# Self-attention of a decoder layer: ScalarE empties PSUM for VectorE, and the projections move to other steps

## The chip, the cores and the metric

One core of one Trainium2 chip. The metric is the device time of one execution of the whole program in microseconds: 2352.65 us, the median of three runs (2352.45 to 2359.95).

## The reference

A decoder layer of three sublayers: causal self-attention with rotary embedding, a cross-attention that gathers, and a quantised gated feed-forward, each followed by a layer norm without weights. Only self-attention is touched. In f32, with x of 4 batches, 1024 tokens, 256 channels and 16 heads of 64:

```
q = (x @ wq.T + bq)  split into 16 heads of 64;  k, v likewise
q, k = rope(q, k)                      # pairs of even and odd channels turned
scores = q k^T, -inf above the diagonal
attn = softmax(scores / 8)
out = (attn @ v) @ wo.T + bo
x = layernorm(x + out)
```

## The kernel before

The work of self-attention (`attention`, L110) is cut into 16 groups (4 batches by 4 groups of 4 heads), and a group into two pairs of heads; there are 32 pairs n, and p = n % 2 is the pair's place in its group i. p = 0 is called the even pair, p = 1 the odd one. The two heads of a pair lie on the two halves of the partitions.

For a pair TensorE computes, in f32, the transposed scores of 12 units of 128 keys by up to 512 queries (`scores`, L439), adds minus the row maximum by a one-row bf16 matmul (`shift`, L447), ScalarE takes the exponential into one of four buffers (`exponentials`, L543), GpSimd zeroes the part above the diagonal (`mask_probs`, L796) and adds the probabilities up for the denominators (`add_probs`, L814 and L817), and TensorE multiplies them by the values (`weigh`, L463). A pair has 6 steps m of two units each; `weigh` lags one step behind.

The row maximum must be known before. While pair n runs, TensorE computes the scores of pair n + 1 once more, untransposed, in 9 chunks of up to 512 columns per head (`max_chunk`, L417); VectorE adds a mask to the diagonal blocks (L664) and reduces each chunk (`maximum`, L670 and L675), combines and negates (`negate`, L681, L684), TensorE spreads the result into a row (`max_row`, L429) and ScalarE copies it to `bias` (`copy_row`, L532). That copy is where a pair begins in this text.

The projections for group i + 1 also run within group i: four q/k units in the even pair (`project_qk`, L360 to L364, three products of high and low f32r parts), two value units in the odd pair (`project_v`, L385 to L387), and the output projection of group i - 1 in the odd pair (`project_out`, L401). Every q/k unit is 128x1024 (even and odd channels, 512 tokens). VectorE adds the bias and multiplies by cosine and sine in four operations reading PSUM (`rotate`, L608) into `turned` and `crossed`; GpSimd subtracts and adds the two (`turn`, L833, L834); SP restacks `turned` by DMA into the operands of the next pair (`stack`, L280). VectorE copies the values out with their bias (`values`, L649) and adds the output projection to y (`residual`, L711). Weights and x are loaded into three `raw` buffers (L266) and split by VectorE into high and low parts (`split`, L614, L616). The denominators go through PSUM (`sums`, L475), a ScalarE copy (L557) and two DMAs that ScalarE issues (L562), are inverted by VectorE and broadcast by SP, and VectorE normalises (`normalise`, L697).

What orders this: each engine's queue is written out by hand over n and m, with the same tables CHUNKS_AT (which chunks in which step) and FULL_AT (which projection in which step). PSUM has a ring of three slots of two banks, taken in the order of `slot_order`, and a separate slot for the outputs. A use of a slot waits until the use three places earlier has been read (`wait_slot`):

```
            elif kind == "max":
                pe.wait_ge(s_mread, PARTS * (NCH * n + u + 1))
            elif kind == "qk":
                pe.wait_ge(s_term, TERMS * (QK_UNITS * n + u + 1))
```

so a chunk's slot waits for VectorE's reduction and a q/k unit's for VectorE's rotation, a score's for its exponential, the row's for ScalarE's copy.

Of the kernel before, what the change touches and what calls it, by code (L numbers as in the profile page):

```python
# [17 lines left out]
P = 128  # L18
# [13 lines left out]
CHUNKS = [[(0, 0), (2, 0)], [(3, 0)], [(1, 0), (5, 1)], [(4, 0)], [(5, 0)], [(6, 0)], [(7, 0)], [(4, 1), (6, 1)], [(7, 1)]]  # L32
# [3 lines left out]
CHUNKS_AT = [range(0, 0), range(0, 3), range(3, 5), range(5, 7), range(7, 9), range(0, 0)]  # L36
# [36 lines left out]
def slot_order():  # L73

    order = [("qk", 0, u) for u in range(QK_UNITS)] + [("v", 0, u) for u in range(V_UNITS)]
    order += [("max", 0, c) for c in range(NCH)] + [("row", 0, 0)]
    for n in range(PAIRS):
        i, p = divmod(n, 2)
        for m in range(STEPS):
            order += [("s", n, 2 * m), ("s", n, 2 * m + 1)]  # L80
            if n + 1 < PAIRS:
                order += [("max", n + 1, c) for c in CHUNKS_AT[m]]
# [6 lines left out]
            if m == 1 and n:  # L89
                order.append(("den", n - 1, 0))  # L90
            if m == STEPS - 1 and n + 1 < PAIRS:
                order.append(("row", n + 1, 0))
# [4 lines left out]
def split_order():  # L97

    order = [("x", 0, piece) for piece in range(X_PIECES)] + [("qk", 1, kt) for kt in range(KT)]
    for i in range(GROUPS):  # L100
        if i + 1 < GROUPS:
            order.append(("v", i + 1, 0))
        if i + 2 < GROUPS:
            order += [("qk", i + 2, kt) for kt in range(KT)]
# [5 lines left out]
def attention(nc, dram, y, psum):  # L110

    ctx = ExitStack()
    with ctx:
# [13 lines left out]
        bv = sb("bv", [P, GC])  # L127
# [10 lines left out]
        crossed = [sb(f"crossed{n}", [P, 2, BANK]) for n in range(2)]  # L138
# [3 lines left out]
        vals = [sb(f"vals{n}", [P, TT, GH, D]) for n in range(2)]  # L142
        maxes = sb("maxes", [P, 2, TT + TT // 2])
# [13 lines left out]
        out_bias = sb("out_bias", [P, E])  # L157
        a_stats = sb("a_stats", [P, TT, 6])
# [16 lines left out]
        s_bv = sem("bv_loaded")  # L175
# [6 lines left out]
        s_qk_done = sem("qk_projected")  # L182
        s_term = sem("rotary_terms")
# [3 lines left out]
        s_m = sem("max_scores")  # L187
        s_mmask = sem("max_chunks_masked")
# [35 lines left out]
        def wait_slot(pe, kind, n, u):  # L224
# [28 lines left out]
        def _(sp):  # L253
# [14 lines left out]
            def load_v_bias(i):  # L268

                if i:  # L270
                    sp.wait_ge(s_vals, V_UNITS * i)
# [67 lines left out]
        def _(pe):  # L339
# [145 lines left out]
            for c in range(NCH):  # L485
                max_chunk(0, c)
# [1854 lines left out]
```

## Time and profile before

| | us |
|---|---|
| median of the runs | 2352.65 |
| the profiled execution | 2353.15 |
| its span, first to last instruction | 2351.4 |
| self-attention, up to about | 1500 |
| mean granted TensorE clock | 0.907 of full |

Busy over the span: TensorE 81%, VectorE 66%, GpSimd 58%, ScalarE 39%. "Idle before" an instruction is the time its engine stood still ahead of it, and the arrow names the instruction that released it. The fraction PEclk is the granted clock of TensorE, 1.00 being 2.4 GHz and 0.5 being 1.2 GHz. Matmul ends are modelled, so a stretch of TensorE is best read from start to start.

### The profile page before, as it was taken

How to read it: one execution, taken by the hardware profiler on the slowest of the kernel's cores; microseconds unless marked ns; L12 is line 12 of the kernel's file. 1: busy time of each engine (PE TensorE's matmuls, PEld its weight loads, DVE VectorE, ACT ScalarE, POOL GpSimd, SP SyncE). 2: the span in 40 equal slices, each digit the busy share in tenths (PEclk: the TensorE clock that was granted, in tenths of full speed). 3: DMA queues.
4: the chain of work that ended last, by engine and by line, in shares of the span. 5: the costliest groups of instructions: out<-in, count | busy, mean ns of one | idle time of the engine just before them, and what ended most of it. 6: DMA issues, size and time to landing. Idle time of an engine off the chain costs nothing. (4 is left out here: it accounts for less than half of the span.)

```text
span 2351.4 us, 41565 instructions
## 1 busy us (share of the span) xinstructions
PE 1910.8 (81%) x16891; PEld 1149.5 (49%) x16891; DVE 1551.9 (66%) x2339; ACT 912.5 (39%) x1273; POOL 1352.3 (58%) x1066
## 2 busy tenths in 40 slices
PE   6898988898879889887998888658788788784575
PEld 3444445445445454444454454436566566563332
DVE  5666665656766656666557664167868868768676
ACT  0222222222222222222222223137675765874375
POOL 2666656756846766766568466235555454646247
PEclk8999989999989999998999999779898898998786
DMA  7022112212221221222122111200000000100002
GB/s 209 19 53 50 48 46 57 61 35 55 62 50 48 53 50 48 52 52 59 32 57 61 32 48 33 66 6 8 2 3 7 2 2 2 41 3 2 2 1 72
DMA packets 59087, 93.34 MB, mean 40 GB/s; under 512 B 25360, under 2 KB 37648, under 8 KB 54928
## 3 DMA queue, kind: packets, MB, share of 16 engines
q1 hardware_dynamic: 49680, 90.41, 15.4%
q8 instruction: 134, 2.20, 0.4%
q10 hardware_dynamic: 9216, 0.27, 0.2%
q14 instruction: 57, 0.47, 0.1%
HBM read 52.37 MB, written 4.46 MB: 24 GB/s over the span
## 5 line engine op out<-in xcount | busy, mean ns | idle before, releaser
L817 POOL TENSOR_TENSOR acc<-acc,probs 128x1024 f32<-128x1024 f32 (+3 forms) x320 | 567.5, 1774 | 103.6 <-ACT probs L543 74.8
L543 ACT ACTIVATE probs<-psum 128x1024 f32<-128x1024 f32 (+3 forms) x384 | 291.2, 812 | 611.4 <-PE psum L447 610.5
L670 DVE TENSOR_REDUCE maxes<-psum 128x2 f32<-128x1024 f32 (+1 forms) x224 | 268.4, 1223 | 197.0 <-PE psum L417 187.2
L439 PE MATMUL psum<-operands 64*128 64x512 f32 (+3 forms) x1536 | 327.2, 537 | 26.9 <-DVE maxes L675 23.4
L1375 ACT ACTIVATE onehot<-psum 128x1024 bf16<-128x1024 f32 x320 | 323.9, 1041 | 1.3 <-PE psum L1185 1.3
L463 PE MATMUL psum<-probs,vals 128*64 128x512 f32 (+3 forms) x1536 | 291.9, 501 | 17.2 <-issue 12.8
L1203 PE MATMUL psum<-pieces,onehot 128*128 128x64 bf16 x7680 | 287.3, 198 | 22.9 <-ACT vs L1382 16.9
L1203 PEld LDWEIGHTS psum<-pieces,onehot 128*128 128x128 bf16 x7680 | 258.9, 101 | 84.8 <-issue 44.9
L1782 POOL TENSOR_TENSOR vs<-vs,wgt 128x1280 f32<-128x1280 f32 x64 | 156.3, 2442 | 247.0 <-DVE wgt L1626 246.9
L814 POOL COPY acc<-probs 128x1024 f32<-128x1024 f32 x64 | 67.9, 1062 | 331.6 <-ACT probs L543 331.6
L439 PEld LDWEIGHTS psum<-operands 64*128 64x128 f32 x1536 | 133.9, 192 | 172.7 <-issue 104.6
L664 DVE TENSOR_TENSOR psum<-psum,later 128x512 f32<-128x512 f32 (+1 forms) x160 | 94.0, 587 | 184.5 <-PE psum L417 184.5
L1185 PE MATMUL psum<-i0T,near 32*128 32x512 bf16 x640 | 130.4, 407 | 83.3 <-ACT onehot L1375 77.3
L1592 DVE TENSOR_TENSOR prod<-psum,xq 128x320 f32<-128x320 f32 x256 | 124.2, 489 | 108.3 <-PE psum L1203 102.9
L796 POOL TENSOR_SCALAR_AFFINE_SELECT probs<-probs 128x256 f32<-128x256 f32 x256 | 123.4, 498 | 105.6 <-ACT probs L543 105.1
L463 PEld LDWEIGHTS psum<-probs,vals 128*64 128x64 f32 x1536 | 95.2, 137 | 164.2 <-issue 141.2
L401 PE MATMUL psum<-wo,ctxT 128*128 128x256 f32 x512 | 145.9, 448 | 34.4 <-DVE maxes L675 22.8
L557 ACT ACTIVATE rden<-psum 128x1024 f32<-128x1024 f32 x32 | 32.8, 1025 | 360.7 <-PE psum L475 360.7
L1382 ACT ACTIVATE vs<-psum 128x320 f32<-128x320 f32 x256 | 115.5, 451 | 144.8 <-DVE prod L1592 144.2
L417 PE MATMUL psum<-operands 64*128 64x512 f32 (+3 forms) x768 | 113.0, 398 | 53.2 <-DMA operands<-turned 46.0
L401 PEld LDWEIGHTS psum<-wo,ctxT 128*128 128x128 f32 x512 | 114.2, 229 | 61.6 <-DVE maxes L675 26.0
L417 PEld LDWEIGHTS psum<-operands 64*128 64x128 f32 x768 | 62.6, 195 | 136.8 <-issue 64.1
(222 smaller groups left out, 3315.6 us busy)
## 6 DMA issues: line engine op xcount, KB each, us to landing
operands<-turned SPq DMA_DIRECT2D x124, 256.0 KB, 4.4
rden<-inverse_rows SPq DMA_DIRECT2D x64, 256.0 KB, 3.9
raw<-in_wqk SPq DMA_DIRECT2D x30, 256.0 KB, 5.2
y<-in_x SPq DMA_DIRECT2D x1, 4096.0 KB, 18.8
wo<-in_wo SPq DMA_DIRECT2D x16, 256.0 KB, 2.6
out<-res SPq DMA_DIRECT2D x16, 256.0 KB, 2.1
raw<-in_wv SPq DMA_DIRECT2D x15, 256.0 KB, 5.0
raw<-in_xT SPq DMA_DIRECT2D x12, 256.0 KB, 3.6
```

The costliest lines, as they stand in the source:

```text
L401: last = nc.tensor.matmul(dst[:, t // 2, (t % 2) * E:(t % 2 + 1) * E], ctxT[:, ct, tok:tok + P], wo[:, ct, :], start=ct == 0, stop=ct == C ...
L417: last = nc.tensor.matmul(dst[:, hh, col:col + width], ops[p][rows, 0, qt * P:(qt + 1) * P], ops[p][rows, 1, hf * BANK:hf * BANK + width], ...
L439: nc.tensor.matmul(dst[:, hh, 0:width], ops[n % 2][rows, 1, kt * P:(kt + 1) * P].bitcast(F32), ops[n % 2][rows, 0, a:a + width].bitcast(F3 ...
L463: last = nc.tensor.matmul(obank[rows, hf, a - hf * BANK:BANK], vals[i % 2][:, kt, 2 * p + hh, :], probs[u % PBUF][:, hh, 0:width], start=k ...
L543: nc.scalar.activation(probs[u % PBUF][:, :, 0:width], slot("s", n, u)[:, :, 0:width], ACT.Exp, scale=1.0 / D ** 0.5).then_inc(s_exp, 1)
L670: V.reduce_max(maxes[:, :, place_of[0]:place_of[-1] + 1:step], src[:, :, 0:len(parts) * width].rearrange("p h (k q) -> p h k q", q=width), ...
L817: G.tensor_tensor(dst, dst, src, ALU.add).then_inc(s_acc, 1)
L1185: last = nc.tensor.matmul(bc[m % 2][:, hf * BANK:(hf + 1) * BANK], near[row:row + Q, NK * j + k, :], i0T[row:row + Q, hp // 2, :], start=T ...
L1203: last = nc.tensor.matmul(out, onehot[:, n % 2, k, tok:tok + P], pieces[b % 2][p][:, h, :, :].rearrange("p (s c) d -> p s (c d)", s=2), st ...
L1375: A.activation(onehot[:, n % 2, k, :], bc[m % 2], ACT.Relu).then_inc(s_oh, 1)
L1592: V.tensor_tensor(prod[u % 2][:, :, :].rearrange("p t (k d) -> p t k d", d=HD), slot("s", n, u)[:, :, 0:W].rearrange("p t (k d) -> p t k d ...
L1782: G.tensor_tensor(v, v, w.broadcast_to([P, TT * NK * 2, HD]), ALU.mult).then_inc(s_wm, 1)
```

## The change

- ScalarE copies every max chunk from PSUM to one of three bf16 buffers in SBUF (`copy_chunk`), every q/k unit to one of two f32 buffers (`stage`), and the values (`values`). The PSUM slots are released by these copies. VectorE masks and reduces the bf16 copies, and rotates out of the staged copy, writing the sine terms back in place; `crossed` is gone.
- The value bias is no longer added to the values: once, at the start, it is multiplied by all of wo (8 matmuls) and added to the output bias. The load of the value bias for each group is gone; the start loads all of wo (1 MB) and spreads the bias over 128 columns.
- q/k units run in steps 0, 1, 4, 5 of the even pair (before 1, 2, 3, 4), values in steps 4, 5 of the odd pair (before 2, 3). In step 1 the chunks come behind projection and sums. The chunks with a masked block come first; steps 1 to 4 have 2, 2, 2, 3 of them.
- GpSimd turns q/k unit 3 at the head of the odd pair. VectorE splits the q/k weights in step 0 and the value weights in step 1 of the odd pair (before steps 4 and 0). Projections wait only for the half of x that they read; at a batch change three pieces of x are loaded in one place and the fourth behind the next stack of operands.

```
-CHUNKS = [[(0, 0), (2, 0)], [(3, 0)], [(1, 0), (5, 1)], [(4, 0)], [(5, 0)], [(6, 0)], [(7, 0)], [(4, 1), (6, 1)], [(7, 1)]]
+CHUNKS = [[(0, 0), (2, 0)], [(3, 0)], [(1, 0), (5, 1)], [(4, 1), (6, 1)], [(7, 1)], [(4, 0)], [(5, 0)], [(6, 0)], [(7, 0)]]
-CHUNKS_AT = [range(0, 0), range(0, 3), range(3, 5), range(5, 7), range(7, 9), range(0, 0)]
+CHUNKS_AT = [range(0, 0), range(0, 2), range(2, 4), range(4, 6), range(6, 9), range(0, 0)]
-FULL_AT = [[None, ("qk", 0), ("qk", 1), ("qk", 2), ("qk", 3), None],
-           [("out", 0), ("out", 1), ("v", 0), ("v", 1), None, None]]
+FULL_AT = [[("qk", 0), ("qk", 1), None, None, ("qk", 2), ("qk", 3)],
+           [("out", 0), ("out", 1), None, None, ("v", 0), ("v", 1)]]
+CHUNKS_LAST = 1
+MBUF = 3
...
             elif kind == "max":
-                pe.wait_ge(s_mread, PARTS * (NCH * n + u + 1))
+                pe.wait_ge(s_mcopy, NCH * n + u + 1)
...
             elif kind == "qk":
-                pe.wait_ge(s_term, TERMS * (QK_UNITS * n + u + 1))
+                pe.wait_ge(s_stage, QK_UNITS * n + u + 1)
...
+            def copy_chunk(n, c):
+                k = NCH * n + c
+                act.wait_ge(s_m, k + 1)
+                if k >= MBUF:
+                    act.wait_ge(s_mread, PARTS * (k + 1 - MBUF))
+                nc.scalar.activation(chunks[k % MBUF][:, :, :], slot("max", n, c)[:, :, :], ACT.Copy).then_inc(s_mcopy, 1)
+            def stage(i, u):
+                m = QK_UNITS * i + u
+                act.wait_ge(s_qk_done, m + 1)
+                if m >= 2:
+                    act.wait_ge(s_rot, TURNS * (m - 1))
+                nc.scalar.activation(staged[m % 2][:, :, :], slot("qk", i, u)[:, :, :], ACT.Copy).then_inc(s_stage, 1)
+            def values(i, u):
+                act.wait_ge(s_v_done, V_UNITS * i + u + 1)
...
+            def project_value_bias():
+                pe.wait_ge(s_bv, 16 * (NG + 1))
+                pe.wait_ge(s_bvr, 1)
+                wait_slot(pe, "bias", 0, 0)
+                dst = slot("bias", 0, 0)
+                for k in range(NG * CT):
+                    last = nc.tensor.matmul(dst[:, 0, 0:E], bv_rep[:, k, :], wo_all[:, k, :],
+                                            start=k == 0, stop=k == NG * CT - 1)
...
-                for dst, x, b, table in ((tu[:, 0, :], ev, be, cosE), (tu[:, 1, :], od, bo, cosO),
-                                         (co[:, 0, :], od, bo, sinE), (co[:, 1, :], ev, be, sinO)):
+                for dst, x, b, table in ((tu[:, 0, :], ev, be, cosE), (tu[:, 1, :], od, bo, cosO)):
                     V.scalar_tensor_tensor(out=dst, in0=x, scalar=b, in1=table[:, tok], op0=ALU.add, op1=ALU.mult)\
+                     .then_inc(s_term, 1)
+                dve.wait_ge(s_term, TERMS * m + 2)
+                for x, b, table in ((ev, be, sinO), (od, bo, sinE)):
+                    V.scalar_tensor_tensor(out=x, in0=x, scalar=b, in1=table[:, tok], op0=ALU.add, op1=ALU.mult)\
                      .then_inc(s_term, 1)
...
+                    if p == 1 and m == 0 and i + 1 < GROUPS:
+                        turn(i + 1, QK_UNITS - 1)
                     for u in (2 * m, 2 * m + 1):
                         if u in DIAGONAL:
                             mask_probs(n, u)
```

## Rows read from the trace of the kernel before

**Rows 1.** The page: busy time over the span.

```profile
PE 1910.8 (81%) x16891; PEld 1149.5 (49%) x16891; DVE 1551.9 (66%) x2339; ACT 912.5 (39%) x1273; POOL 1352.3 (58%) x1066
```

**Rows 2.** Busy time by stretch: even pair, odd pair, batch change, start; clock, DMA.

```profile
core 0: us, PE busy (x) PEld busy (x) DVE busy (x) ACT busy (x) POOL busy (x), PEclk, DMA share, GB/s
501.48:543.85 42.37, 37.48 (x218) 19.51 (x218) 30.89 (x40) 12.01 (x16) 32.10 (x28) 1.00 0.21 54
543.85:590.21 46.36, 42.05 (x250) 24.06 (x251) 28.83 (x46) 12.12 (x16) 26.15 (x22) 0.93 0.21 46
681.67:734.70 53.03, 40.69 (x218) 21.83 (x218) 39.48 (x48) 12.01 (x16) 33.77 (x28) 0.87 0.25 63
0.00:51.11 51.11, 30.15 (x106) 16.45 (x106) 32.25 (x47) 1.29 (x2) 11.79 (x18) 0.85 0.73 215
```

**Rows 3.** Timeline of TensorE in the even pair: start us, us, instruction, idle before.

```profile
510.32 0.47 PE L360 MATMUL psum<-xT_high,wqk_high 128*128 128x512 f32 x1 [1.75 <-DVE maxes L675]
...
543.18 0.64 PE L429 MATMUL psum<-ident,negmax 128*64 128x128 bf16 x16 [2.00 <-DVE crossed L608]
```

**Rows 4.** Timeline of TensorE in an odd pair, two stalls.

```profile
459.68 3.72 PE L401 MATMUL psum<-wo,ctxT 128*128 128x256 f32 x16
...
469.33 5.20 PE L401 MATMUL psum<-wo,ctxT 128*128 128x256 f32 x16 [1.65 <-DVE maxes L675]
...
498.44 0.49 PE L439 MATMUL psum<-operands 64*128 64x128 f32 x4 [1.47 <-DVE maxes L675]
```

**Rows 5.** Timeline of TensorE behind the 2.00 us stall.

```profile
543.75 3.11 PE L439 MATMUL psum<-operands 64*128 64x512 f32 x8
```

**Rows 6.** Timeline of TensorE, step 3 of the even pair and the next scores.

```profile
522.76 1.99 PE L439 MATMUL psum<-operands 64*128 64x512 f32 x8
...
527.64 0.50 PE L360 MATMUL psum<-xT_high,wqk_high 128*128 128x512 f32 x1
...
530.57 1.77 PE L439 MATMUL psum<-operands 64*128 64x512 f32 x8
```

**Rows 7.** ScalarE: 128x1024 from PSUM (busy us, mean ns); issue of the two DMAs.

```profile
L543 ACT ACTIVATE probs<-psum 128x1024 f32<-128x1024 f32 x186 | 184.0, 1024 | 419.6 <-PE psum L447 419.6
...
516.27 1.13 ACTq L562 DMA_DIRECT2D dcol<-rden  x2
```

**Rows 8.** VectorE: chunk maximum and rotation terms by shape.

```profile
L670 DVE TENSOR_REDUCE maxes<-psum 128x2 f32<-128x1024 f32 x192 | 229.3, 1223 | 193.7 <-PE psum L417 187.2
...
L608 DVE SCALAR_TENSOR_TENSOR crossed<-psum,bqk,rot 128x512 f32<-128x512 f32 x128 | 89.6, 742 | 0.0
```

**Rows 9.** Timeline of VectorE: operations from SBUF, without and beside GpSimd.

```profile
31.97 0.69 DVE L616 TENSOR_TENSOR xT_low<-acc,xT_high 128x512 fp32r<-128x512 f32 x1
...
49.74 0.20 DVE L684 TENSOR_SCALAR negmax<-maxes 128x16 bf16<-128x16 f32 x1
...
504.32 1.21 DVE L697 TENSOR_TENSOR ctxT<-osum,rden 128x1024 f32<-128x1024 f32 x1
...
539.19 1.25 DVE L684 TENSOR_SCALAR negmax<-maxes 128x16 bf16<-128x16 f32 x1
...
545.54 1.63 DVE L616 TENSOR_TENSOR wv_low<-raw,wv_high 128x512 fp32r<-128x512 f32 x1
```

**Rows 10.** Timeline of GpSimd at the same times.

```profile
534.77 4.36 POOL L817 TENSOR_TENSOR acc<-acc,probs 128x1024 f32<-128x1024 f32 x2
539.09 1.28 POOL L833 TENSOR_TENSOR turned<-turned,crossed 128x512 f32<-128x512 f32 x1
...
545.19 1.44 POOL L833 TENSOR_TENSOR turned<-turned,crossed 128x512 f32<-128x512 f32 x1
546.59 1.72 POOL L834 TENSOR_TENSOR turned<-turned,crossed 128x512 f32<-128x512 f32 x1
```

**Rows 11.** Timeline at a batch change: the stack's issue on SP, the chunk on TensorE.

```profile
687.48 3.64 SPq L280 DMA_DIRECT2D operands<-turned  x4
...
695.83 1.76 PE L417 MATMUL psum<-operands 64*128 64x128 f32 x10 [8.01 <-DMA operands<-turned]
```

More of the change, by code:

```diff
@@ L75, in slot_order @@
     order = [("qk", 0, u) for u in range(QK_UNITS)] + [("v", 0, u) for u in range(V_UNITS)]
-    order += [("max", 0, c) for c in range(NCH)] + [("row", 0, 0)]
+    order += [("max", 0, c) for c in range(NCH)] + [("bias", 0, 0), ("row", 0, 0)]
     for n in range(PAIRS):
@@ L79, in slot_order @@
         for m in range(STEPS):
+            chunks = [("max", n + 1, c) for c in CHUNKS_AT[m]] if n + 1 < PAIRS else []
             order += [("s", n, 2 * m), ("s", n, 2 * m + 1)]
-            if n + 1 < PAIRS:
-                order += [("max", n + 1, c) for c in CHUNKS_AT[m]]
+            if m != CHUNKS_LAST:
+                order += chunks
             if FULL_AT[p][m]:
@@ L90, in slot_order @@
                 order.append(("den", n - 1, 0))
+            if m == CHUNKS_LAST:
+                order += chunks
             if m == STEPS - 1 and n + 1 < PAIRS:
@@ L100, in split_order @@
     for i in range(GROUPS):
+        if i + 2 < GROUPS:
+            order += [("qk", i + 2, kt) for kt in range(KT)]
         if i + 1 < GROUPS:
             order.append(("v", i + 1, 0))
-        if i + 2 < GROUPS:
-            order += [("qk", i + 2, kt) for kt in range(KT)]
         if i % NG == 2 and i // NG + 1 < B:
@@ L137, in attention @@
         turned = sb("turned", [P, 2, 2, S])
-        crossed = [sb(f"crossed{n}", [P, 2, BANK]) for n in range(2)]
+        staged = [sb(f"staged{n}", [P, 2, BANK]) for n in range(2)]
         ops = [sb(f"operands{n}", [P, 2, S], F32R) for n in range(2)]
@@ L142, in attention @@
         vals = [sb(f"vals{n}", [P, TT, GH, D]) for n in range(2)]
+        chunks = [sb(f"chunks{n}", [P, 2, BANK], BF16) for n in range(MBUF)]
         maxes = sb("maxes", [P, 2, TT + TT // 2])
@@ L486, in _ @@
                 max_chunk(0, c)
+            project_value_bias()
             max_row(0)
@@ L515, in _ @@
                         sums(n - 1)
+                    if m == CHUNKS_LAST and n + 1 < PAIRS:
+                        for c in CHUNKS_AT[m]:
+                            max_chunk(n + 1, c)
                     if m == STEPS - 1 and n + 1 < PAIRS:
@@ L563, in spread_sums @@
                        .then_inc(s_dcol, 16)
+            for u in range(QK_UNITS):
+                stage(0, u)
+            for u in range(V_UNITS):
+                values(0, u)
+            for c in range(NCH):
+                copy_chunk(0, c)
             copy_row(0)
             for n in range(PAIRS):
+                i, p = divmod(n, 2)
                 for m in range(STEPS):
@@ L571, in _ @@
                         copy_out(n - 1, 1)
+                    if m != CHUNKS_LAST and n + 1 < PAIRS:
+                        for c in CHUNKS_AT[m]:
+                            copy_chunk(n + 1, c)
+                    if FULL_AT[p][m] and i + 1 < GROUPS:
+                        kind, u = FULL_AT[p][m]
+                        if kind == "qk":
+                            stage(i + 1, u)
+                        if kind == "v":
+                            values(i + 1, u)
                     if m == 1 and n:
                         spread_sums(n - 1)
+                    if m == CHUNKS_LAST and n + 1 < PAIRS:
+                        for c in CHUNKS_AT[m]:
+                            copy_chunk(n + 1, c)
                     if m == 3:
@@ L733, in _ @@
                 rotate(0, u)
-            for u in range(V_UNITS):
-                values(0, u)
             for piece in range(X_PIECES):
@@ L769, in _ @@
                             rotate(i + 1, u)
-                        if kind == "v" and i + 1 < GROUPS:
-                            values(i + 1, u)
+                    if m == CHUNKS_LAST and n + 1 < PAIRS:
+                        for c in CHUNKS_AT[m]:
+                            maximum(n + 1, c)
                     if p == 1 and m == STEPS - 1 and i % NG == 2 and i // NG + 1 < B:
-                        for piece in range(2):
+                        for piece in range(KT):
                             split_x(i // NG + 1, piece)
                     if p == 0 and m == 0 and i % NG == 3 and i // NG + 1 < B:
-                        for piece in range(2, X_PIECES):
+                        for piece in range(KT, X_PIECES):
                             split_x(i // NG + 1, piece)
```

106 lines of the change are left out of this document (58 added, 48 removed).

## The prediction

> **What bounds the kernel now.** I read the page first: TensorE is busy 81% of the span, ScalarE 39% [rows 1]. The change lies wholly in self-attention, so the next view is busy time by stretch, between the copies of the maximum row (L532) with which each head pair begins [rows 2]. A pair that projects q and k for the next group (an even pair) takes 42.37 us, with TensorE busy 37.48. The odd one after it, with output and value projections, takes 46.36 us, busy 42.05 at a mean clock of 0.93. VectorE and GpSimd are busy about 30 us of each, ScalarE 12. TensorE is the bound, and it stands still 4.9 and 4.3 us of the two pairs. A group of two pairs lasts 88.73 us; 15 groups project for a successor.
>
> TensorE's timeline shows where it stands. In the even pair the first projection waits 1.75 us for VectorE's maximum of the chunk in its PSUM slot, and the maximum row waits 2.00 us for the rotation of the last q/k unit, whose slot it reuses [rows 3]. In the odd pair an output projection waits 1.65 us and a score 1.47 us, again for maxima [rows 4]. So every larger stall is a PSUM slot that VectorE has not read. Idleness also costs clock: behind the 2.00 us stall eight score matmuls take 3.11 us [rows 5] where the same eight take 1.77 elsewhere [rows 6], which is half clock (1.2 instead of 2.4 GHz) for a few us. The output projection behind the 1.65 us stall takes 5.20 us [rows 4], one before it 3.7. With the shift behind the scores (0.4) that is 1.3 + 0.4 + 1.5 = 3.2 us of a group.
>
> **The floor.** Without stalls the even pair is its busy time, 37.5. The odd one is 42.05 less 3.2 of slow clock, 38.9. Floor 76.4 us for a group.
>
> **ScalarE's new work and what it makes late.** Nine chunk copies, on average two q/k stages and one value copy come to a pair: 12 copies of 128x1024 from PSUM at 1.02 us [rows 7], 12.3 us on top of 12, so 24 of 40: no bound by amount. But its queue is in order, and TensorE's slots now hang on it. Take time from the end of the second projection (step 1, even pair). The sums take 1.94 us; ScalarE copies them by 2.97, then issues two DMAs, 1.13 us [rows 7], and copies the first chunk by 5.15. TensorE has run sums, two chunks (1.02) and one score (0.9) by 3.86, and its second score needs that chunk's slot: stall 1.3. The exponentials of that step end near 8.45, TensorE wants their slot at 8.2: 0.25. In step 4 q/k unit 2 waits for the copy of the chunk three places ahead: 0.45. Sum 2.0 us a pair, odd pairs likewise. Steps 2 and 3 keep no projection: 7.81 us less 2.93 leaves 4.9 [rows 6], against 4.1 us of ScalarE. The maximum row's slot is now that of an exponential and is free; the copies of the last stage and of the row (2.04 us) lie beside row and scores (2.4). So 76.4 + 4.0 = 80.4 us a group.
>
> **VectorE and GpSimd.** Values leave VectorE (1.2 us each). A maximum reads bf16 in SBUF instead of PSUM, 1.23 us now [rows 8]; I take no more than 0.1 off. The rotation is the doubtful part. Its four operations now take 0.74 us reading PSUM and a table [rows 8]; changed, they read two SBUF tensors. The trace has no such operation; the nearest row is the split's subtraction of the same 128x512, 0.69 us with GpSimd idle [rows 9]. Yet beside GpSimd the same shape takes 1.63 us, and GpSimd's turns 1.44 and 1.72 instead of 1.28 [rows 9, 10]. And a 16-element scaling, 0.20 us alone, takes 1.25: it ends just after the GpSimd turn that began before it [rows 9, 10]. So where both want SBUF, one waits for the other's instruction to end. The change puts 16 rotation terms a group into this conflict.
>
> Price: GpSimd has 32 us in an even pair [rows 2]; 16 rotation terms add at most 0.57 each, 9 us, masks and normalisation 2.5: 43.5 us, begun 3 us into the pair. GpSimd turns unit 3 at the head of the next pair, before it masks that pair's first probabilities. TensorE wants those masks 7.6 us into the odd pair (step 0: scores and shift 2.1, products 0.8, output projection 3.7; step 1: scores and shift 1.1), 47.4 us from the even pair's start, with 39.8 for that pair. Every lock collected: 46.5, plus the mask 0.8 and idleness in step 2, 49 to 51; and VectorE (last chunk reduced and negated by 36.9, unit 2 rotated between GpSimd's additions by 41.6, normalised by 43.9, unit 3 by 47.8) has two splits of q/k weights (2.2 us alone, some 6 in turns with GpSimd) before the residual that frees the output slot: near 55 us where TensorE comes at 49.1. All locks: stall 6. No lock: unit 3 is staged 0.5 us into the odd pair, rotated by 3.3, turned by 5.9, masked by 6.7, in time: stall 0. GpSimd is busy three quarters of an even pair, and a term that meets it meets it anywhere in an instruction, so I take the middle, 3 us. A stall of this size had a half-clock stretch behind it before [rows 3, 5]: 1.6 us. Group 85.0 us, saving 3.7; 15 groups, 56 us.
>
> **Batch changes.** Three pairs of the kind of 681.7 to 734.7 take 53.0 instead of 42.4 us [rows 2]. The stack of operands is issued at 687.5 behind the loads of x, the chunk waits 8.01 us for it, and the pair runs at 0.87 of the clock [rows 11]. Now three pieces are loaded at a time when their buffers are free, the fourth behind the stack, and only units 2 and 3 need it. Its split falls between two rotations, 1 to 2 us. Saving 9 each, 27 us.
>
> **Start and end.** Before the first pair lie 51.1 us, VectorE busy 32 [rows 2]. Added: a stage copy 1 us, locks between rotations and turns 4, bias spreading 1.2, eight f32 matmuls and an addition 3.5, chunk copies and 1 MB more of DMA ahead of the operands 0 to 5; removed: values, 2.4. I take 8 longer, 3 to 14 as ends. The last two pairs gain 2. The bias loads that leave SP's queue were hidden, and the output bias is read a group later. The weights' loads change places (q/k before v), as their splits do; all have most of a pair to land, so nothing is counted, and if one were late, a projection would wait its 5 us.
>
> Sum: 56 + 27 + 2 - 8 = 77 us less. The profiled execution is 2353.15 us, 0.5 above the median of the three runs. Forecast 2276 us.
>
> **Rivals.**
> A, the port costs nothing on the path (0.22): turn and masks are in time, group 80.4, saving 125 + 27 + 2 - 8 = 146: 2207. For it: VectorE rests about 12 us of a pair, and the terms need not fall beside additions. Against: [rows 9].
> B, every lock is collected (0.18): a term waits out the addition in front of it, late masks and the late residual hold TensorE 6 us of a group, slow clock behind: 88.0. Batch changes, with two more splits between rotations, save 5 each instead of 9: 11 + 15 + 2 - 8 = 20 less: 2333. For it: [rows 9]. The Trainium skill, "SBUF — State Buffer", section "Who interferes with whom", gives this case as its rule: VectorE and GpSimd share a pair of ports under an exclusive lock held for the whole instruction, and two SBUF inputs on VectorE contend with GpSimd's reads. By that rule, the trace agrees, the time is nearer this one.
> C, slower (0.11): a rotation term from SBUF takes not 0.69 but about 1.21 us, what the normalisation of twice as many elements takes [rows 9]. 16 times 0.52 is 8.3 us, all on VectorE and the port in the even pair, where both are full: group 93.3, 69 us lost, 21 won by the other terms: 2401. It decides from 5.1 us more in a group, a term of 1.01 us. No row has this operation from SBUF. The Trainium skill, "Vector Engine (DVE) Microarchitecture Reference", section "Points that are easy to get wrong", says that such an operation with two non-bf16 SBUF sources runs at half throughput; no run here shows it.
> D (0.04): ScalarE's queue frees slots no sooner than VectorE's did, groups stay at 88.7 to 89, and the start eats the batch changes: 2350.
>
> **How the numbers follow.** My forecast has 0.45. A measurement of this kernel can tell 0.3%, 7 us. Faster: 0.45 + 0.22 + 0.18 = 0.85; same 0.04; slower 0.11. The range takes in the start's ends, A's and B's: 2200 to 2345; C, D and the tails stay outside.
>
> **What would show it.** Even pairs near 40 us and odd ones near 45; TensorE's waits for VectorE's maxima gone, in their place one of about 1.3 us in step 2 for ScalarE's copy; ScalarE busy about 24 us a pair; rotation terms of 0.69 us alone and 1 to 2 us beside GpSimd; in the odd pair a wait of the probability products (L463) for GpSimd's mask, half clock behind it; batch changes near 44. Rotation terms of 1.2 us without GpSimd, or an even pair above 42, would make me wrong. Turns done under 6 us into the odd pair would mean A.

## The result, and the profile after

The changed kernel takes 2282.41 us, the median of four runs (2280.27 to 2285.43). The kernel before took 2352.55 beside it, also four runs. The ratio is 0.970, with a 95% interval of 0.9678 to 0.9723: 3.0% faster, 70 us. The forecast was 2276, with a range of 2200 to 2345. The profiled execution took 2283.46 us, its span 2281.6; 69.8 of the 70 us lie between the two spans.

The page, busy time over the span; before it was [rows 1]:

```profile
PE 1881.6 (82%) x16902; PEld 1121.2 (49%) x16907; DVE 1679.5 (74%) x2309; ACT 1276.4 (56%) x1657; POOL 1398.6 (61%) x1066
```

ScalarE gained 364 us, VectorE 128, though the values left VectorE, and GpSimd 46, though it does the same work. TensorE lost 29 us with all but the same matmuls (the changed kernel has 11 more records), so it ran less at half clock: the mean granted clock of the profiled execution is 0.926, before it was 0.907.

Busy time by stretch, of the changed kernel: all 31 stretches between maximum rows, an even pair, the odd pair before it, a pair at a batch change, the start (columns as in [rows 2]):

```profile
54.58:1382.31 1327.73, 1189.53 (x7082) 637.88 (x7083) 1002.99 (x1075) 722.08 (x864) 937.81 (x746) 0.98 0.22 51
...
477.72:517.73 40.01, 37.36 (x218) 19.26 (x216) 29.82 (x32) 24.43 (x31) 29.77 (x25) 1.00 0.14 37
...
432.01:477.72 45.71, 40.60 (x250) 22.75 (x248) 32.65 (x33) 22.45 (x29) 30.32 (x24) 0.96 0.28 62
...
306.17:346.19 40.02, 37.37 (x218) 19.26 (x216) 32.57 (x36) 24.43 (x30) 29.96 (x25) 1.00 0.16 44
...
0.00:54.58 54.58, 35.50 (x122) 21.08 (x123) 36.86 (x46) 16.21 (x16) 14.58 (x18) 0.84 0.68 207
```

The same 31 stretches lasted 1401.0 us before (51.11 to 1452.14), so they gave 73.3 us; the start took 3.5 back. I took the length of every pair from the copies of the maximum row in both traces:

| pairs | before, us | after, us | won |
|---|---|---|---|
| 12 even ones | 42.9 mean | 40.2 mean | 32.2 |
| 3 even ones at a batch change | 52.7, 53.0, 53.2 | 40.0, 40.0, 41.3 | 37.6 |
| 14 odd ones from the second on | 46.72 mean | 46.65 mean | 0.9 |
| first odd pair | 43.0 | 40.4 | 2.6 |

The last of the 31 stretches, an even pair that projects nothing, takes 30 us in both, and so does what lies behind the last maximum row (899.3 us). Nearly all of the gain is in even pairs. The odd ones, 43.6 to 50.7 us long, gave next to nothing from the second on: ten of the fourteen won 10.3 us together, and the four longest (49.4, 50.7, 49.6 and 47.6) lost 9.4. The timeline of one of the ten on TensorE in the changed kernel (start us, us, instruction, idle before):

```profile
441.63 3.26 PE L488 MATMUL psum<-probs,vals 128*64 128x512 f32 x8 [2.46 <-issue]
444.82 3.75 PE L415 MATMUL psum<-wo,ctxT 128*128 128x256 f32 x16
...
451.56 1.13 PE L464 MATMUL psum<-operands 64*128 64x512 f32 x4 [0.42 <-ACT rden L610]
...
453.85 1.13 PE L464 MATMUL psum<-operands 64*128 64x512 f32 x4 [1.16 <-ACT chunks L570]
...
457.23 2.04 PE L464 MATMUL psum<-operands 64*128 64x512 f32 x8 [0.29 <-ACT probs L596]
...
467.92 0.36 PE L399 MATMUL psum<-wv_high,xT_high 128*128 128x256 f32 x1 [0.75 <-ACT chunks L570]
...
471.97 1.72 PE L488 MATMUL psum<-probs,vals 128*64 128x512 f32 x8
```

No wait for a maximum is left. At 441.63 the products of probabilities and values wait 2.46 us, and then take 3.26 us where the same eight take 1.72: half clock (1.2 instead of 2.4 GHz; the granted clock over them is 0.50, and 1.00 over the other eight). The profile names no releaser for this wait ("issue"). What it waits for is read from GpSimd's timeline in the same kernel, and the first experiment tests it:

```profile
431.99 2.19 POOL L904 TENSOR_TENSOR turned<-turned,staged 128x512 f32<-128x512 f32 x1 [1.29 <-DVE staged L679]
...
437.94 1.38 POOL L904 TENSOR_TENSOR turned<-turned,staged 128x512 f32<-128x512 f32 x1 [2.08 <-DVE staged L679]
439.28 1.71 POOL L905 TENSOR_TENSOR turned<-turned,staged 128x512 f32<-128x512 f32 x1
440.94 1.40 POOL L867 TENSOR_SCALAR_AFFINE_SELECT probs<-probs 128x256 f32<-128x256 f32 x2
```

GpSimd turns unit 2 and then unit 3, and masks at 440.94. It waits 2.08 us for VectorE's terms of unit 3, whose own timeline in the changed kernel is:

```profile
432.97 3.43 DVE L675 SCALAR_TENSOR_TENSOR turned<-staged,bqk,rot 128x512 f32<-128x512 f32 x2
436.44 1.42 DVE L679 SCALAR_TENSOR_TENSOR staged<-staged,bqk,rot 128x512 f32<-128x512 f32 x2
438.23 1.64 DVE L687 TENSOR_TENSOR wqk_low<-raw,wqk_high 128x512 fp32r<-128x512 f32 x1
442.00 1.21 DVE L782 TENSOR_TENSOR y<-y,psum 128x1024 f32<-128x1024 f32 x1
```

The first of GpSimd's two masks ends near 441.6, where TensorE goes on. Two cosine terms beside GpSimd's turn of unit 2 (432 to 435.9) take 3.43 us; two sine terms with GpSimd idle take 1.42. The average over all, groups of VectorE by shape in the changed kernel (busy us, mean ns | idle before):

```profile
L740 DVE TENSOR_REDUCE maxes<-chunks 128x2 f32<-128x1024 bf16 x192 | 223.6, 1215 | 11.2 <-ACT chunks L570 4.2 <-DVE chunks L734 0.5
L675 DVE SCALAR_TENSOR_TENSOR turned<-staged,bqk,rot 128x512 f32<-128x512 f32 x128 | 156.5, 1262 | 184.4 <-ACT staged L578 178.0 <-DMA operands<-turned 6.4
L734 DVE TENSOR_TENSOR chunks<-chunks,later 128x512 bf16<-128x512 bf16 x96 | 129.1, 1345 | 105.5 <-ACT chunks L570 105.5
L679 DVE SCALAR_TENSOR_TENSOR staged<-staged,bqk,rot 128x512 f32<-128x512 f32 x128 | 116.4, 949 | 2.3
```

A term was 742 ns out of PSUM [rows 8]. Out of SBUF the quickest is 744 and the mean 1262 and 949; the line's own summary (quickest/mean/slowest ns) shows the spread:

```profile
L675 DVE SCALAR_TENSOR_TENSOR turned<-staged,bqk,rot x120: 744/962/1852, 62.3 to 1311.3; 128x512 f32<-128x512 f32 x120
```

### The profile page after: what moved, and what is told of

It is laid out like the page before. It is cut to its first block and busy times, and to the rows that moved or that the text cites. A ratio compares the mean times of both kernels' runs of the same rounds, so it can differ in the third digit from the quotient of the medians.

```text
span 2281.6 us, 42244 instructions
## 1 busy us (share of the span) xinstructions
PE 1881.6 (82%) x16902; PEld 1121.2 (49%) x16907; DVE 1679.5 (74%) x2309; ACT 1276.4 (56%) x1657; POOL 1398.6 (61%) x1066
## 5 line engine op out<-in xcount | busy, mean ns | idle before, releaser
L888 POOL TENSOR_TENSOR acc<-acc,probs 128x1024 f32<-128x1024 f32 (+3 forms) x320 | 578.3, 1807 | 42.1 <-ACT probs L596 13.6
L464 PE MATMUL psum<-operands 64*128 64x512 f32 (+3 forms) x1536 | 318.2, 519 | 54.9 <-ACT chunks L570 34.6
L488 PE MATMUL psum<-probs,vals 128*64 128x512 f32 (+3 forms) x1536 | 305.0, 519 | 42.7 <-issue 38.1
L570 ACT ACTIVATE chunks<-psum 128x1024 bf16<-128x1024 f32 x288 | 278.2, 1025 | 91.2 <-PE psum L431 46.8
L1274 PEld LDWEIGHTS psum<-pieces,onehot 128*128 128x128 bf16 x7680 | 263.7, 102 | 88.8 <-issue 46.1
L675 DVE SCALAR_TENSOR_TENSOR turned<-staged,bqk,rot 128x512 f32<-128x512 f32 x128 | 156.5, 1262 | 184.4 <-ACT staged L578 178.0
L740 DVE TENSOR_REDUCE maxes<-chunks 128x2 f32<-128x1024 bf16 (+1 forms) x224 | 262.7, 1216 | 14.5 <-ACT chunks L570 4.2
L734 DVE TENSOR_TENSOR chunks<-chunks,later 128x512 bf16<-128x512 bf16 (+1 forms) x160 | 169.3, 1058 | 105.5 <-ACT chunks L570 105.5
L464 PEld LDWEIGHTS psum<-operands 64*128 64x128 f32 x1536 | 127.0, 185 | 190.0 <-ACT chunks L570 106.8
L578 ACT ACTIVATE staged<-psum 128x1024 f32<-128x1024 f32 x64 | 65.6, 1025 | 179.8 <-PE psum L378 158.9
L415 PE MATMUL psum<-wo,ctxT 128*128 128x256 f32 x512 | 127.9, 406 | 27.4 <-DVE y L782 15.9
L904 POOL TENSOR_TENSOR turned<-turned,staged 128x512 f32<-128x512 f32 x64 | 100.9, 1577 | 68.5 <-DVE staged L679 68.5
```

Of the source, the lines that this page charges most:

```text
L464: nc.tensor.matmul(dst[:, hh, 0:width], ops[n % 2][rows, 1, kt * P:(kt + 1) * P].bitcast(F32), ops[n % 2][rows, 0, a:a + width].bitcast(F3 ...
L488: last = nc.tensor.matmul(obank[rows, hf, a - hf * BANK:BANK], vals[i % 2][:, kt, 2 * p + hh, :], probs[u % PBUF][:, hh, 0:width], start=k ...
L570: nc.scalar.activation(chunks[k % MBUF][:, :, :], slot("max", n, c)[:, :, :], ACT.Copy).then_inc(s_mcopy, 1)
L675: V.scalar_tensor_tensor(out=dst, in0=x, scalar=b, in1=table[:, tok], op0=ALU.add, op1=ALU.mult)\
L734: V.tensor_tensor(block, block, mask, ALU.add).then_inc(s_mmask, 1)
L740: V.reduce_max(maxes[:, :, place_of[0]:place_of[-1] + 1:step], src[:, :, 0:len(parts) * width].rearrange("p h (k q) -> p h k q", q=width), ...
```

## The experiments

All are edits of the changed kernel unless said otherwise. Ratios are to the kernel before, run beside them. My theory: in the odd pair, locks make unit 3's terms late, GpSimd masks behind them, and VectorE's residual, behind two weight splits, is next in line. Rivals: the copies on ScalarE are themselves the cost, or the staging's lock isn't what makes the terms late.

**Masks before the turn of unit 3.**

```
-                    if p == 1 and m == 0 and i + 1 < GROUPS:
-                        turn(i + 1, QK_UNITS - 1)
                     for u in (2 * m, 2 * m + 1):
                         ...
+                    if p == 1 and m == 0 and i + 1 < GROUPS:
+                        turn(i + 1, QK_UNITS - 1)
```

> The changed kernel, but GpSimd masks the first two units of the odd pair before it turns q/k unit 3. In the changed kernel the products (L488) of the odd pair wait 2.46 us for these masks and then run at half clock (3.26 instead of 1.72 us). Theory: the wait for the masks goes, but VectorE, late by the same locks, frees the output slot only at 11.2 us into the pair, where TensorE would arrive at 8.9; so a wait of about 2.3 us for the residual (L782) stands in its place and the pair gains about 1.5 us: 14 pairs, about 20 us, 2262. Rival (the masks alone hold the pair): 2.5 + 1.5 us from each odd pair, 2226. Rival (the turn must come first, since the stack behind it becomes late): no gain or slower, with waits of L431 for the operands.

2314.69 us, ratio 0.983 (0.9813 to 0.9842): 32 us slower than the changed kernel. The mask's wait is gone, and another has come. Waits of TensorE from 60 to 1380 us (total, times, longest), first of the changed kernel, then of this one:

```profile
PE psum L488 <- issue: 38.1, 15, 4.8
...
PE psum L415 <- DVE y L782: 15.9, 7, 3.7
```

```profile
PE psum L415 <- DVE y L782: 71.1, 14, 7.1
```

Its timeline on TensorE:

```profile
453.15 6.53 PE L415 MATMUL psum<-wo,ctxT 128*128 128x256 f32 x16 [3.24 <-DVE y L782]
```

The output projection waits for the residual, which here ends at 453.10, 12.0 us into the pair (from 441.09), where in the changed kernel it ended 11.2 us in: VectorE's second split, which now meets the copy that begins GpSimd's additions (450.19 to 451.42), takes 1.41 us instead of 0.77, and the sine terms before it 1.58 instead of 1.42. And TensorE, freed of its first wait, comes earlier. Then sixteen matmuls take 6.53 us instead of 3.75, at a granted clock of 0.56. The order of the two holds was as I thought; that removing one hold would gain was wrong. I had expected a wait of 2.3 us; the fourteen are 5.1 in the mean, and the longest, 7.1, stand in the four pairs with row scalings. The rival, a stack that becomes late, isn't it: only one chunk waits for its operands, 8.2 us.

**Rotation out of PSUM again (no staging; chunks still copied).**

```
-                ev, od = staged[m % 2][:, 0, :], staged[m % 2][:, 1, :]
+                src, co = slot("qk", i, u), staged[m % 2]
+                ev, od = src[:, 0, :], src[:, 1, :]
```

> The changed kernel, but the rotation reads q/k from PSUM as before and writes its sine terms into the SBUF buffer; ScalarE stages nothing, the slot is released by the rotation. Theory (the rotation's two SBUF inputs lock VectorE and GpSimd against each other): terms at 0.74 us everywhere, turn of unit 3 done by 6 instead of 9 us into the odd pair, no wait for the masks; in return a wait of about 1.3 us for the slot of unit 3 at the start of the odd pair. Even pairs 40.3, odd 43 instead of 45.7: about 35 us less, 2247. Rival (staging is what frees the slots in time): odd pairs gain the masks and lose as much at the slots, even pairs back above 41: 2285 to 2310.

2280.14 us, ratio 0.968 (0.9664 to 0.9694): the same as the changed kernel. Its groups of VectorE, its largest wait of TensorE, and two neighbouring pairs, odd and even:

```profile
L674 DVE SCALAR_TENSOR_TENSOR turned<-psum,bqk,rot 128x512 f32<-128x512 f32 x118 | 83.0, 744 | 205.9 <-PE psum L378 205.9
```

```profile
PE psum L374 <- DVE staged L677: 30.9, 15, 2.3
```

```profile
438.84:481.97 43.13, 39.59 (x250) 22.46 (x252) 27.64 (x31) 22.44 (x27) 26.61 (x22) 1.00 0.31 65
481.97:525.65 43.68, 38.80 (x218) 20.41 (x215) 27.21 (x33) 20.56 (x26) 30.79 (x26) 0.96 0.13 34
```

The mean term is 744 ns again, the quickest one of the staged kernel: reading both inputs from SBUF beside GpSimd is what lengthened it. But for the first two, odd pairs fall to 43.1 to 44.7 and even ones rise to 42.0 to 44.7, because the projections wait once more for slots that the rotation reads. Neither number on record was met: the gain in odd pairs was as my theory had it, the loss in even pairs as the rival had it. Staging gives in even pairs what it costs in odd ones.

**Maxima out of PSUM again (no chunk copies; staging kept).**

```
-                pe.wait_ge(s_mcopy, NCH * n + u + 1)
+                pe.wait_ge(s_mread, PARTS * (NCH * n + u + 1))
...
-                src = chunks[k % MBUF]
+                src = slot("max", n, c)
```

> The changed kernel, but VectorE masks and reduces the chunks in PSUM as before, and ScalarE copies no chunk. Theory (the order of chunks and projections is what removed the waits, not the copies): the chunk slots are read by VectorE just before TensorE returns to them, the masks no longer wait for GpSimd (1.06 us mean now), even pairs 39.5 to 40.5, odd as now or 1 us less: 2260 to 2285. Rival (the copies pay): TensorE again waits 1.5 to 2 us for maxima in every pair, half clock behind some, even pairs 42: 2320 or more.

2366.49 us, ratio 1.005 (1.0032 to 1.0070): all of the gain is lost. Waits of TensorE in this kernel:

```profile
PE psum L464 <- DVE maxes L737: 58.6, 29, 5.5
PE psum L464 <- DVE maxes L732: 40.5, 58, 1.0
```

The slots of the chunks now wait for VectorE, which the rotation out of SBUF makes late. That the staging does this is shown by the kernel without either (two experiments on): it differs from this one in the staging alone and takes 2280 us.

**ScalarE issues its two DMAs behind the chunk copies of the step.**

```
+            def send_sums(n):
...
                     if m == CHUNKS_LAST and n + 1 < PAIRS:
                         for c in CHUNKS_AT[m]:
                             copy_chunk(n + 1, c)
+                    if m == 1 and n:
+                        send_sums(n - 1)
```

> The changed kernel, but ScalarE issues its two DMAs (1.13 us) behind the copies of the two chunks of step 1 instead of before them. Theory (TensorE's 1.16 us wait of step 2 for the first chunk's copy is this issue): the wait goes in all pairs, even pairs 40.0 to 38.9, odd the same less: 30 pairs, 30 to 35 us, 2248. Rival (TensorE then waits for the next exponentials or copies instead, as ScalarE's queue holds the same work): under 10 us, 2275.

2245.63 us, ratio 0.954 (0.9516 to 0.9557), 37 us less than the changed kernel. An even pair of this kernel, and TensorE where the changed kernel waited 1.16 us:

```profile
468.03:506.68 38.65, 37.16 (x218) 19.26 (x216) 29.70 (x32) 24.32 (x30) 29.78 (x25) 1.00 0.14 38
```

```profile
443.24 2.04 PE L464 MATMUL psum<-operands 64*128 64x512 f32 x8
```

In the changed kernel these eight scores were twice four. ScalarE's own timeline there, with the issue ahead of the copies:

```profile
451.54 1.13 ACTq L615 DMA_DIRECT2D dcol<-rden  x2
452.77 1.94 ACT L570 ACTIVATE chunks<-psum 128x1024 bf16<-128x1024 f32 x2 [1.26 <-issue]
```

With the issue moved, the 15 even pairs won 17 us (1.35 in the plain ones; the first is longer) and the 15 odd ones 17. The one shown above fell from 45.7 to 42.8, and half of that is not the wait: its stall for the masks is again 2.46 us, but is followed by full clock here,

```profile
434.87 1.73 PE L488 MATMUL psum<-probs,vals 128*64 128x512 f32 x8 [2.46 <-issue]
```

where the changed kernel took 3.26.

**Order of work alone: neither staging nor chunk copies.** Both edits of the second and third experiment together; values on ScalarE, bias folding and the steps as changed.

> The changed kernel without staging and without chunk copies: the new order of chunks, projections and loads, the values on ScalarE and the value bias through the output bias remain. Theory (order pays, copies only bring locks): the port conflict is that of the kernel before, even pairs near 40, odd 42 to 43: 2235 to 2255, faster than the changed kernel. Rival (the slots need ScalarE): waits for maxima and rotations add up to 3 us and more a pair: 2320 to 2350.

2279.95 us, ratio 0.968 (0.9652 to 0.9700): the same as the whole change. An odd and an even pair of this kernel:

```profile
441.55:485.80 44.25, 39.80 (x250) 22.45 (x252) 25.81 (x32) 13.98 (x18) 27.71 (x24) 1.00 0.29 64
485.80:527.07 41.27, 37.44 (x218) 19.18 (x215) 25.15 (x33) 12.10 (x17) 28.92 (x25) 1.00 0.13 36
```

So the copies that head the change earn nothing in it. With neither copy it is 2280 us, with chunk copies alone 2280, with staging alone 2366, with both 2282. The 3% come from what is left: the order of the work, the loads at a batch change, the value copy and the folded bias. Which of these brings them wasn't taken apart, but that the loads alone bring nothing (next). My theory, that the kernel would be faster without the copies (2235 to 2255), missed, and so did the rival (2320 and more).

**Batch-change loads alone, in the kernel before.** The piecewise loads of x and waits for half of x, and nothing else.

```
-                    for piece in range(X_PIECES):
+                    for piece in range(X_PIECES - 1):
...
+                if i % NG == 3 and i // NG + 1 < B:
+                    load_piece("x", i // NG + 1, X_PIECES - 1)
```

> The kernel before with nothing but the batch change's loads: the fourth piece of x is loaded behind the next stack of operands, and projections wait only for their half of x. Theory: the wait of 8.0 us for the stack goes at three batch changes, 24 to 31 us less: 2325. Rival (VectorE's splits of x hold the same pair anyway): 0 to 10 us less, 2345 to 2352.

2352.22 us, ratio 0.998 (0.9966 to 1.0000): nothing. The three pairs take 52.1, 51.0 and 51.1. SP's queue in this kernel and in the changed one:

```profile
300.44 16.61 SPq L266 DMA_DIRECT2D raw<-in_xT  x3
317.09 3.67 SPq L280 DMA_DIRECT2D operands<-turned  x4
```

```profile
296.00 1.53 SPq L281 DMA_DIRECT2D raw<-in_xT  x3
```

SP is stuck 16.6 us at the three pieces, until VectorE has split the q/k weights whose `raw` buffers they take; the last of these splits ends at 316.69. The stack of operands stands behind them. In the changed kernel these splits lie in step 0 of that odd pair and not in step 4, and the three issues take 1.53 us. So the piecewise loads don't bring the gain of 12.5 us a batch change by themselves. Whether the earlier splits alone would wasn't tried. And the copies have a share in it: in the kernel with the new order alone, which has both edits, the three pairs still take 45.1, 44.3 and 44.9, where its plain even pairs take 41.3.

**The residual of the first output unit before the q/k splits.**

```
+                    if p == 1 and m == 0 and i:
+                        residual(i - 1, 0)
                     if p == 1 and m == 0 and i + 2 < GROUPS:
                         for kt in range(KT):
                             split_qk(i + 2, kt)
```

> The changed kernel, but VectorE adds the residual of output unit 0 before it splits the q/k weights and normalises rows, in step 0 of the odd pair. In five of the odd pairs TensorE's second output projection waited about 3 us for this residual and ran at half clock (6.52 instead of 3.72 us). Theory: this wait goes in those pairs, the wait for the masks (2.46 us) stays in all: 2282 less about 20 to 25, 2260; the other odd pairs stay at 45 to 46. Rival (the splits, now later, hold the residual of unit 1 instead): 2280 or more.

2254.04 us, ratio 0.956 (0.9550 to 0.9579), 28 us less than the changed kernel. The odd pair of the earlier timelines stays at 45.3 us. The four that hold row scalings of the layer norm (L799) besides the q/k splits, both ahead of the residual before, fall from 49.4, 50.7, 49.6 and 47.6 to 43.6, 44.6, 43.6 and 43.6. One of the four in this kernel:

```profile
606.17:649.76 43.59, 39.04 (x250) 22.38 (x248) 39.16 (x41) 22.44 (x28) 30.72 (x24) 1.00 0.36 82
```

In the changed kernel it showed on TensorE

```profile
614.06 1.73 PE L488 MATMUL psum<-probs,vals 128*64 128x512 f32 x8 [2.46 <-issue]
619.50 5.14 PE L415 MATMUL psum<-wo,ctxT 128*128 128x256 f32 x16 [3.71 <-DVE y L782]
```

that is, both holds, with slow matmuls behind the second. Four pairs wait 2.4 to 3.7 us for the residual in the changed kernel, not five as I had written, and three more wait about 1 us.

**Both holds away, and the rest of VectorE's odd pair later.** Masks first, residual first, value splits in step 2, row scaling in step 3.

> The changed kernel with both holds of the odd pair taken away together: GpSimd masks before it turns unit 3, VectorE adds the residual first, splits the value weights in step 2 and normalises rows in step 3. Theory (masks behind the turn and residual behind the splits are one hold, the lock's lateness, seen from two engines; each alone gains nothing because the other stands behind it): odd pairs 41 to 42, group 82: 14 times 4 and the longer pairs' 3 to 5 more, 2210. Rival (VectorE and GpSimd are at their limit by amount, the lateness moves to the next slot, value split or chunk masks): 2250 to 2280.

2229.00 us, ratio 0.947 (0.9445 to 0.9486). Odd pairs are 41.6 to 42.7 us but for three of 46.1 to 47.1. An odd pair and the waits of TensorE in this kernel:

```profile
423.50:465.12 41.62, 38.79 (x250) 22.42 (x248) 32.97 (x33) 22.55 (x28) 32.07 (x24) 1.00 0.31 68
```

```profile
PE psum L431 <- DMA operands<-turned: 35.0, 15, 8.3
```

The first edit alone lost 32 us, the second won 28, and together with the moves they won 53. The turn is late now, so the stack lands late, and one chunk waits for it.

**The same with ScalarE's DMAs later.**

> The kernel of e10_odd_free (masks before the turn, residual first, later value splits and row scaling) with ScalarE's DMA issues behind the chunk copies, as in e4_dma_later. The changed kernel was 2282, e10 2229 (even pairs 40.0, odd 41.6), e4 2246 (even 38.65). Theory (the two gains are of different waits, 1.35 us of each pair and the odd pair's hold, and add up in the even pairs; in the odd ones the stack of operands, which is late in e10, takes the place of what the DMA issue frees): even 38.7, odd 41.0 to 41.6, 2229 less 20 to 30: 2203. Rival (they add up fully): odd 40.3, 2190. Rival (later sums make the normalisation late): 2220 or more.

2211.51 us, ratio 0.940 (0.9375 to 0.9421): 17.5 us less, even pairs 38.7.

**The same order without staging and chunk copies** (the order-alone kernel with masks first, residual first and the two moves).

> The kernel of e5_order_alone (no staging, no chunk copies; even pairs 41.3, odd 44.3; 2280) with the odd pair's changes of e10_odd_free. In e5 nothing waits for the masks or the residual; the waits are for slots that VectorE reads late (1.2 us for q/k unit 3, 0.3 to 1 us for maxima). Theory: where no lock makes VectorE and GpSimd late, these moves gain little, 0 to 1 us of an odd pair: 2265 to 2280, so that ScalarE's copies are worth 40 us and more only once the odd pair is freed. Rival (the hold of the odd pair has nothing to do with the locks): 45 to 55 us less, as from the changed kernel to e10: 2230.

2289.50 us, ratio 0.973 (0.9708 to 0.9758): no gain, 10 us more than order alone. Odd pairs stay at 44.3, and three rise to 48.1 to 48.7; these three hold the row statistics and account for the loss. Its largest wait:

```profile
PE psum L464 <- DVE maxes L730: 37.2, 61, 1.0
```

Without copies TensorE is held by its PSUM slots, and freeing masks and residual doesn't help.

**Both holds away, DMAs later, chunk copies kept, rotation out of PSUM.**

> The kernel of e11_odd_dma with the rotation reading PSUM, as in e2_rot_psum: chunk copies stay. Theory (staging buys slots at the price of locks; with the lock's hold cured otherwise, staging pays): q/k slots are held by the rotation, even pairs 41 to 42, odd 41 to 42: 2225 to 2245, slower than e11. Rival (the locks cost more than the slots even now): 2190 or less, faster than e11.

2256.40 us, ratio 0.959 (0.9571 to 0.9607). That is 45 us more than with staging, and 33 less than with no copies at all (a kernel that has the DMAs in their old place as well). The difference to staging lies in the even pairs, 42.2 us in the mean instead of 39.0; the odd ones are alike, 43.0 and 43.1. So staging, which was worth nothing in the changed kernel, is worth 45 us once nothing waits for the terms it delays: it keeps its gain in even pairs and no longer pays for it in odd ones.

**Row statistics in steps 3 and 4 instead of 0 and 1**, on top of the kernel with both holds away and the DMAs later.

```
-                    if p == 1 and m < 2 and i >= NG and i % NG == 1:
-                        row_statistics(i // NG - 1, m)
+                    if p == 1 and 3 <= m < 5 and i >= NG and i % NG == 1:
+                        row_statistics(i // NG - 1, m - 3)
```

> The kernel of e11_odd_dma (2211) with VectorE's row statistics of a finished batch in steps 3 and 4 of the odd pair instead of 0 and 1. Three odd pairs (of the groups 5, 9, 13) still take 46.2 to 46.8 us where the others take 41.5 to 43. Theory: the statistics and their neighbours hold the residual of output unit 1 and with it a chunk's slot; moved, these pairs come down to 42 to 43: 10 to 13 us less, 2200. Rival (the bias additions at a batch's first residual hold them, which stay): 0 to 4 us less, 2209.

2202.81 us, ratio 0.935 (0.9319 to 0.9377), 80 us less than the change itself and the fastest of all. The three pairs with statistics go from 46.4, 46.2 and 46.8 to 42.1, 43.4 and 43.5. An even pair and such an odd pair of this kernel:

```profile
463.43:502.08 38.65, 37.17 (x218) 19.25 (x216) 29.71 (x32) 24.32 (x31) 29.79 (x25) 1.00 0.14 38
...
502.08:544.17 42.09, 38.78 (x250) 22.41 (x248) 38.78 (x51) 22.66 (x29) 33.48 (x25) 1.00 0.31 67
```

TensorE stands still 1.5 us of the even pair and 3.3 of the odd one; before it was 4.9 and 4.3 [rows 2].

## Why the prediction was right

2276 was forecast and 2282 measured. The mechanism was the one given: freed slots in even pairs, a wait for the masks with half clock behind it in odd ones. That the sum came within 7 us is in part luck, since an error of 14 us in the odd pairs is made up in part by 4 us in the even ones and 4.5 at the start. Term by term, with the forecast of 85.0 us for a group split into its two pairs (39.8 and 45.2):

| us won | forecast | measured |
|---|---|---|
| 15 even pairs, batch changes with them | 38.6 + 27 | 69.8 |
| 15 odd pairs | 17.4 | 3.5 |
| start | -8 | -3.5 |
| last pairs and what follows | 2 | 0 |
| sum | 77 | 69.8 |

- **Floor and ScalarE.** Even pairs of 39.8 us were forecast, 40.0 came. The wait of the second score for a chunk copy was 1.3 forecast and 1.16 measured; that the DMA issue ahead of it makes it was shown by moving the issue: the wait went, and 37 us with it. The waits of the odd pair sum to 0.42 + 1.16 + 0.29 + 0.75 = 2.6 us, where I had 2.0.
- **The rotation term.** Taken at 0.69 us from the split's subtraction, it is 0.74 alone. Rival C had 1.21 and fell. The Trainium skill, "Vector Engine (DVE) Microarchitecture Reference", section "Points that are easy to get wrong", expects half throughput for two SBUF sources that aren't bf16. Beside the same operation out of PSUM the runs show no such loss: 744 ns out of SBUF, 742 out of PSUM.
- **The shared port.** Forecast as 1 to 2 us beside GpSimd, measured up to 1.85, and gone when the terms read PSUM. The rule of the Trainium skill's "SBUF — State Buffer", section "Who interferes with whom", agrees with this; the time, which I had called nearer to rival B by that rule, is 6 us from the forecast and 51 from B. GpSimd lost less than I had set as its bound, 11.5 us a group: 46 us over all, 2.9 a group.
- **The mask of the chunks.** This I left out. It now also reads two SBUF tensors, and in bf16: 0.42 us alone, 1.35 in the mean of all, against 0.70 in PSUM (the line below, of the kernel before). Over 96 of them that is 62 us of VectorE. I had priced only the maximum's move, at up to 0.1 us less; it was 1215 instead of 1223 ns, nothing.

```profile
L664 DVE TENSOR_TENSOR psum<-psum,later 128x512 f32<-128x512 f32 x96 | 66.8, 696 | 184.5 <-PE psum L417 184.5
```

- **The odd pair.** A wait of 3 us for GpSimd's mask and 1.6 of half clock were forecast; 2.46 and 3.26 - 1.72 = 1.5 were measured in the pair shown, 45.7 long where I had 45.2. The step that failed is that I carried this pair to all 15. Four have row scaling and q/k splits ahead of the residual, take both holds and reach 47.6 to 50.7. The other ten from the second on won 1.0 each, nearly the 1.2 forecast, and the four lost it again. (A fifth pair with row scaling, the last odd one, has no q/k splits and takes 43.6.)
- **Batch changes.** The sum has 9 us each on top of the 2.6 of an even pair, 11.6, and 12.5 came. By that sum such a pair would take 41.4 us; the "near 44" among the signs doesn't fit it, and 40.0 to 41.3 were measured. The reason was half of it: SP waits for buffers that the q/k splits free, so their earlier place most likely bears on it beside the piecewise load; no run has it alone. I had said of the splits' new place that nothing was to be counted for it.
- **The start.** 8 us longer was forecast, 3.5 measured. No experiment takes its parts asunder.
- **Rivals.** A needed turns done under 6 us into the odd pair; they ended 9.0 us in (440.99 - 432.01). B's price of 6 us of stall in every group was met only by the pairs with row scaling and splits (2.46 + 3.71). D fell with the even pairs.

**Where the expected gain went.** Slots freed by copies were to free TensorE. They did in even pairs. In odd ones the rotation out of SBUF was late, and with it the masks and the residual. These two hide each other: the masks' move alone cost 32 us, the residual's alone won 28, both with the two later moves won 53. What exactly in that last kernel each of the two moves brings wasn't tried. Nor are the shares settled of the 32 us that masks first costs alone: the trace shows the later residual and the slow matmuls behind it.

## What to carry to other kernels

Moving an operand of VectorE from PSUM to SBUF frees a PSUM slot, and where the other operand lies in SBUF too, it puts VectorE in line with GpSimd; look for the small operation that queues behind the two (a mask, a residual), since it decides whether the freed slot is worth anything. Where two holds end near each other, remove both before judging either, and judge each half of a change with the other half in place. A DMA issued by a compute engine stands in its queue like an instruction, here 1.1 us on the path in every pair, and belongs behind what another engine waits for.

## What the runs showed of the hardware

- A bf16 mask of 128x512 in SBUF takes 0.42 us alone. I laid the timelines of VectorE and GpSimd in the changed kernel over each other: 33 of the 96 masks meet no GpSimd instruction and take 0.42 to 0.43; the other 63 take 1.83 in the mean, up to 2.57. The f32 cosine terms of the same shape take 0.74 and, 120 of 128 beside GpSimd, 1.30. The shorter operation loses most; why was not tried. VectorE's timeline has both sides:

```profile
453.83 0.42 DVE L734 TENSOR_TENSOR chunks<-chunks,later 128x512 bf16<-128x512 bf16 x1 [4.00 <-ACT chunks L570]
...
458.12 2.02 DVE L734 TENSOR_TENSOR chunks<-chunks,later 128x512 bf16<-128x512 bf16 x1 [1.03 <-ACT chunks L570]
```

- The same comparison for VectorE's other operations: the maximum, whose only large input is in SBUF, takes 1.21 to 1.22 us beside GpSimd (184 of 192) as alone, and so does the residual, with one input in PSUM. The scaling of 16 elements [rows 9], with one input in SBUF, does get longer, so the number of SBUF inputs alone doesn't decide.
- Reducing 1024 bf16 elements from SBUF (1215 ns) is no quicker than 1024 f32 elements from PSUM (1223 ns).
- The same stall doesn't always cost clock. Two odd pairs of the kernel with the residual first, with the same instructions on TensorE around it, both wait 1.91 us:

```profile
443.98 2.83 PE L488 MATMUL psum<-probs,vals 128*64 128x512 f32 x8 [1.91 <-issue]
...
615.25 1.72 PE L488 MATMUL psum<-probs,vals 128*64 128x512 f32 x8 [1.91 <-issue]
```

The granted clock over the first eight matmuls is 0.58, over the second 1.00. In the changed kernel eleven odd pairs wait 2.46 us for the masks; seven go on slowly, four at full clock. So the 1.6 us that I added to every stall of this size is a price of some of them.
